# The third group's depthwise convolution moved from GpSimd to TensorE, in three parts, and the first context moved behind the second keys' transposes

## The reference

```python
q = einsum('oc,bchw->bohw', wq, fmap)                        # 64 -> 128 channels
kdw = conv_general_dilated(fmap, wdw, 3x3, pad 1, groups=C)  # depthwise, 9 taps
kv = einsum('oc,bchw->bohw', wpw, kdw)
k, v = split(kv, 2, axis=1)
q = softmax(q, over the 16 channels of a head) * 16 ** -0.5
k = softmax(k, over the 256 pixels)
context = einsum('bnd,bne->bde', k, v)
out = gelu(einsum('bnd,bde->bne', q, context))
return einsum('oc,bchw->bohw', wout, out) + bout[None, :, None, None]
```

## Time and profile before

| | |
|---|---|
| median of three runs | 659.12 us |
| profiled execution | 653.08 us, span 651.3 us |
| TensorE busy | 582.6 us, 89% of the span |
| VectorE busy | 402.6 us, 62% |
| ScalarE busy | 313.8 us, 48% |
| GpSimd busy | 292.3 us, 45% |
| mean granted TensorE clock | 0.937 |

### The profile page before, as it was taken

One profiled execution on the slowest core, in us unless ns is written; L12 is line 12 of the kernel. 1 busy time (PEld: TensorE's weight loads), 2 busy tenths in 40 slices (PEclk: granted clock), 3 DMA queues, 4 the chain that ended last, 5 costly groups with the idle time before them and its releaser, 6 DMA issues.

```text
span 651.3 us, 10438 instructions
## 1 busy us (share of the span) xinstructions
PE 582.6 (89%) x3574; PEld 303.7 (47%) x3574; DVE 402.6 (62%) x1162; ACT 313.8 (48%) x549; POOL 292.3 (45%) x371
## 2 busy tenths in 40 slices
PE   7888794898799999999998787998999999997883
PEld 6675433793232333332334557982333333467652
DVE  6655597666687766866867826744953333445567
ACT  3334675184333343344345635465555555335384
POOL 6601705150253455697697940540425243435263
PEclk9999887588999999999999978999999999997696
DMA  4720000020554424324321000024322232000001
GB/s 118 140 39 2 2 0 2 9 57 5 133 130 103 99 65 111 84 67 117 78 64 34 0 2 1 11 53 124 79 65 65 66 86 44 1 2 2 2 1 66
DMA packets 33045, 34.62 MB, mean 53 GB/s; under 512 B 11304, under 2 KB 20544, under 8 KB 32928
## 3 DMA queue, kind: packets, MB, share of 16 engines
q1 hardware_dynamic: 32992, 33.95, 22.6%
HBM read 32.50 MB, written 1.44 MB: 52 GB/s over the span
## 4 chain that ended last, share of the span: by engine, by line
PE 74%; DVE 13%; POOL 5%; issue 3%; ACT 3%; DMA 1%; SPq 0%; DVEq 0%; ACTq 0%; POOLq 0%
PE ps L1812 10%; PE ps L1849 9%; PE ps L2473 9%; PE ps L2463 8%; PE ps L1804 8%; PE ps L421 4%; PE ps L2573 2%; DVE ST L487 2%; POOL dw_out L1562 2%; PE ps L763 1%; PE ps L2882 1%; PE ps L1202 1%; POOL tap_prod L1572 1%; PE ps L2185 1%; PE ps L1362 1%
## 5 line engine op out<-in xcount | busy, mean ns | idle before, releaser
L1465 POOL TENSOR_TENSOR out_acc<-out_acc,tok_tmp 128x512 f32<-128x512 f32 x88 | 113.7, 1292 | 180.9 <-DVE tok_tmp L1677 90.5
L1744 ACT ACTIVATE act_pair<-ps 128x1024 f32<-128x1024 f32 x64 | 65.5, 1024 | 112.6 <-PE ps L1804 112.6
L1812 PE MATMUL ps<-tokP,w_raw 64*128 64x512 f32 x256 | 73.1, 648 | 1.0 <-DVE tok_split L1671 0.5
L1804 PE MATMUL ps<-tokP,w_raw 64*128 64x512 f32 x256 | 67.4, 603 | 2.4 <-ACT act_pair L1744 2.4
L2463 PE MATMUL ps<-tokP,w 64*128 64x512 f32 x256 | 63.8, 616 | 0.0
L1677 DVE TENSOR_TENSOR tok_tmp<-ps,disp_all 128x512 f32<-128x512 f32 x60 | 41.2, 690 | 25.5 <-PE ps L1849 20.0
L532 ACT ACTIVATE U<-X,nmr,rstd 128x64 f32<-128x64 f32 x120 | 41.8, 429 | 21.1 <-POOL nmr L510 16.6
L2366 DVE SCALAR_TENSOR_TENSOR tok_tmp<-ps,b,disp_all 128x512 f32<-128x512 f32 x28 | 21.0, 750 | 48.4 <-PE ps L2473 39.7
L1671 DVE TENSOR_TENSOR tok_split<-act_pair,ps 128x1024 f32<-128x1024 f32 x32 | 39.1, 1221 | 14.7 <-PE ps L1812 14.4
L2418 ACT ACTIVATE hid_four<-ps,b 128x1024 f32<-128x1024 f32 x32 | 33.9, 1110 | 29.5 <-PE ps L2463 29.5
L1671 DVE TENSOR_TENSOR hid_four<-act_pair,ps 128x1024 f32<-128x1024 f32 x32 | 39.1, 1222 | 13.9 <-PE ps L1812 12.4
(11 more groups left out here) (474 smaller groups left out, 1045.1 us busy)
## 6 DMA issues: line engine op xcount, KB each, us to landing
disp_all<-disp_dram SPq DMA_DIRECT2D x44, 512.0 KB, 6.5
w_raw<-in_L_ffn_w SPq DMA_DIRECT2D x4, 512.0 KB, 9.6
disp_all<-disp_dram SPq DMA_DIRECT2D x4, 384.0 KB, 4.9
XIN<-in_x SPq DMA_DIRECT2D x4, 256.0 KB, 3.3
w_raw<-in_L_ffn_W SPq DMA_DIRECT2D x2, 512.0 KB, 6.1
out<-XIN SPq DMA_DIRECT2D x4, 256.0 KB, 2.2
fc_raw<-in_L_conv_upfc_w SPq DMA_DIRECT2D x1, 512.0 KB, 4.6
w<-in_L_ffn_w SPq DMA_DIRECT2D x1, 512.0 KB, 10.3
```

The source lines that it names most:

```text
L1465: pool.tensor_tensor(out_acc[i % 2][:, :], out_acc[i % 2][:, :], weighed[p % 2], ALU.add).then_inc(mm["acc"].sem, 1)
L1744: act.activation(act_pair[n % 2][:, :], ps[:, 0:2, :].rearrange("p r s -> p (r s)"), ACT.Silu).then_inc(mm["act"].sem, 1)
L1804: last = pe.matmul(ps[:, r, :], w12_raw[half(r), 0, e, :], tokP[half(r), i * CHUNK:(i + 1) * CHUNK], start=True, stop=True)
L1812: last = pe.matmul(ps[:, 2 + r, :], w12_raw[half(r), 1, e, :], tokP[half(r), i * CHUNK:(i + 1) * CHUNK], start=True, stop=True)
```

## The change

Group 2's convolution leaves GpSimd: the 17 steps of `dw_pool(pool, G - 2, n)` go, and `chunk_rstd` follows the experts' last addition directly. TensorE does group 2's nine taps in three parts of 3, 2 and 4 taps, into bank 6. ScalarE moves the sum between the last two `chunk_norm` (`conv_move(G - 2)`), and `keys(2)` waits for that move. Since bank 6 also takes the context, `context(0)` now waits for the move, and stands behind `k_tr(1)`. Group 3's nine taps stand in one piece behind `q_tr(0, 1)`, after `keys(2)` and `values(2)`. The eight matmuls of `keep_clock` go.

```diff
             add_weighed(pool, e1, E1, between, count=G)
-            for n in range(5):
-                dw_pool(pool, G - 2, n)
             for i in (NCHUNK - 2, NCHUNK - 1):
                 chunk_rstd(pool, i, eps_c, m["d_var"], m["d_rstd"])
-            for n in range(5, DW_STEPS):
-                dw_pool(pool, G - 2, n)
...
-                       (G, "d_o_ps d_g d_y_ps d_xo x5"), (3, "d_hm"), (G - 1, "d_kd"), (1, "d_cw d_cv_ps d_kl"), (2 * G, "d_qt_ps d_qt"),
+                       (G, "d_o_ps d_g d_y_ps d_xo x5"), (3, "d_hm"), (G - 2, "d_kd"), (1, "d_cw"), (2, "d_cv_ps d_kl"), (2 * G, "d_qt_ps d_qt"),
...
+            def conv_move(g):
+
+                act.wait_ge(*m["d_cv_ps"](g - 1))
+                act.activation(dw_out[:, g, :], ps[:, 6, :], ACT.Copy).then_inc(m["d_kl"].sem, 1)
+
...
-            for i in (NCHUNK - 2, NCHUNK - 1):
-                chunk_norm(act, i, m["d_rstd"], m["d_u"])
+            chunk_norm(act, NCHUNK - 2, m["d_rstd"], m["d_u"])
+            conv_move(G - 2)
+            chunk_norm(act, NCHUNK - 1, m["d_rstd"], m["d_u"])
...
-            act.wait_ge(*m["d_cv_ps"](1))
-            act.activation(dw_out[:, G - 1, :], ps[:, 6, :], ACT.Copy).then_inc(m["d_kl"].sem, 1)
+            conv_move(G - 1)
...
-                pe.wait_ge(*(m["d_kd"](g + 1) if g < G - 1 else m["d_kl"](1)))
+                pe.wait_ge(*(m["d_kd"](g + 1) if g < G - 2 else m["d_kl"](g - 1)))
...
                 if g == 0:
-                    pe.wait_ge(*m["d_xp"](G - 1))
+                    pe.wait_ge(*m["d_kl"](1))
                 elif g == 1:
-                    pe.wait_ge(*m["d_kl"](1))
+                    pe.wait_ge(*m["d_kl"](2))
...
             values(0)
+            dw_tensor(G - 2, 0, 3)
             experts_back(pe, e1, E1, G - 1)
             k_tr(0)
             q_logits(1)
+            dw_tensor(G - 2, 3, 5)
             keys(1)
             values(1)
-            context(0)
+            dw_tensor(G - 2, 5, 9)
             q_tr(0, 0)
             k_tr(1)
+            context(0)
             pe.wait_ge(*e1["ta"](G + 1))
             pe.wait_ge(*m["d_qt"](1))
             d_tr(pe, G - 1)
             q_logits(2)
-            pe.wait_ge(*m["d_c"](1))
-            keep_clock(pe, 6, 8)
-            q_tr(0, 1)
-            dw_tensor(G - 1, 0, 4)
             keys(2)
             values(2)
-            dw_tensor(G - 1, 4, 9)
+            q_tr(0, 1)
+            pe.wait_ge(*m["d_c"](1))
+            dw_tensor(G - 1, 0, 9)
             context(1)
```

## The result

The changed kernel takes 651.85 us (median of 22 runs, 647.82 to 655.61). The kernel before took 654.13 us (22 runs on the same chip, 651.18 to 660.80); the median of 659.12 that the forecast started from was that of three runs and lay 5.0 us above this one. The ratio is 0.9948, 95% interval 0.9923 to 0.9974: a gain of 3.4 us, between 1.7 and 5.0, where 5.8 was forecast. The difference of the two medians is 2.3 us, that of the two means 3.7 (655.67 and 651.93). The profiled execution took 650.62 us, at a mean granted clock of 0.935 (before: 653.08 at 0.937).

A forecast was written before the change was run, and what follows sets the result against it. GpSimd's convolution of group 2 was taken to bound the stretch before `keys(2)`. 2.7 us from the clock plus 3.1 from GpSimd's wait, less what was added, gave 5.8: 659.12 - 5.8 = 653.3 us, range 651.0 to 656.3.

The forecast's parts named there:

- The stage: From `values(0)` to `context(1)`, rebuilt at full clock: `keys(2)` at 369.3, `context(1)` at 380.3 instead of 386.19, 5.8 us sooner.
- 2.7 come from the clock: From 376.31 to 385.45 TensorE took 9.14 us for work that is 6.41 at full clock.
- From there on the two programs are alike: Behind the start of `context(1)`: nothing differs, so the 5.8 us gained there reach the end.
- the dense order: TensorE's work up to `context(1)`: the forecast's other term, GpSimd's wait less what was added, 3.1 us.
- The argument on the border: Idle 2.10 us ahead of 362.86 brought no clock fall, so the 3.37 us ahead of `k_tr(3)` is near the border.
- The second fall: Rival: the clock fall behind the idle stretch ahead of `k_tr(3)` stays away, 1.7 us more gained, 651.6 us; 15%.
- The waits: Rival: delays on ScalarE's list up to `keys(2)` and in TensorE's list leave 3 to 4 us, about 656 us; 17%.
- the dense stretch: Slower rival: TensorE at 1.2 GHz from `keys(2)` on, 10.1 us more, `context(1)` at 390.4, 663.4 us; 3%.
- The gain reached the end: Rival denied this: something other than this chain gates the next stage, time stays at 659.1 us; 3%.
- GpSimd beside VectorE: Bias additions now beside `q_norm(0)` and `q_center(1)`: a neighbour may cost 0.60 us or nothing; taken as nothing.
- in direction, not in size: L1938's one 1.84 us against its median 1.24, compared with the exclusion rule's possible wait of 1.24 us.
- ScalarE free: After `v_move(2)` and `k_exp(2)`, ahead of group 3's move: free at 378.5, 1.1 us ahead of the taps' end.

The follow-up runs named there:

- before_full: Kernel before with fillers ahead of `k_tr(3)`, behind `context(0)` and behind group 3's first four taps, six routing fillers moved behind the bias products: 649.50 us, ratio 0.9906.
- after_hold: Changed kernel with 13 filler matmuls in the idle 3.38 us between `q_tr(2, 0)` and `k_tr(3)`: 647.72 us, ratio 0.9933 to the kernel before.
- after_both: Changed kernel with 13 filler matmuls ahead of `k_tr(3)` and six routing fillers moved behind the second run of bias products: 647.95 us, ratio 0.9874 to the kernel before.
- after_pool_busy: Changed kernel in which GpSimd still runs the 17 convolution steps, into a spare tile nothing reads: 651.24 us, ratio 0.9956 to the kernel before.
- after_gate: Changed kernel with only six routing fillers moved behind the second run of bias products: 646.96 us, ratio 0.9906 to the kernel before.
- before_filled: Kernel before with 15 filler matmuls behind group 3's first four taps, in the idle 3.75 us ahead of `keys(2)`: 654.85 us, ratio 1.0019.
- before_again: Kernel before run and traced once more, with no edit: ratio 1.0005 to the kernel before.
- before_gate: Kernel before with only six routing fillers moved behind the second run of bias products: 652.99 us, ratio 0.9974.

## Why the prediction was off

**The stage: right.** Forecast and measured starts: `v_move(1)` 360.9 and 361.08; `keys(2)` 369.3 and 369.53; `context(1)` 380.3 and 380.65; `k_tr(3)` 392.9 and 393.15. The clock was full from 350 to 386 us, nothing was idle above 0.78 us, and nine taps took 7.90 us, as priced from the earlier trace rows.

**The step that failed: "2.7 come from the clock", together with "From there on the two programs are alike".** The programs are alike, their clocks are not. I read the first fall of the earlier trace rows as a price that the kernel before pays and the new one does not, and took the clock behind `context(1)` for the same in both. Each of the seven traces of the two unedited kernels has two falls or more (the rows with none are before_full, and after_hold, after_both and after_pool_busy):

| | falls, start in us | sum |
|---|---|---|
| before, four traces | 374.9, 398.8; 375.0, 398.9, 426.2; 365.0, 378.7, 399.1; 363.6, 377.3, 397.8 | 85.7; 90.7; 84.8; 84.7 |
| before, none | none | 81.6 |
| after, three traces | 394.4, 421.7; 394.0, 421.3; 392.2, 419.5 | 82.0; 82.0; 82.1 |
| after, none | none | 78.7 to 78.9 |

Falls cost the kernel before 3.1 to 4.1 us in this part, 9.1 once, and the changed kernel 3.2 to 3.3, three times alike. The changed kernel's are the old fall behind the idle stretch ahead of `k_tr(3)` (1.6: after_gate has it alone, 80.4 against 78.8) and one in the routing that the first trace of before doesn't have (1.6 again: 82.0 against 80.4). So the term put at 2.7 us measured 0 to 1 us against three of the four traces of before, and 5.9 against the fourth. With the 2.8 of the dense order the three make 3 to 4, and the ratio says 3.4 (1.7 to 5.0). The two agree, but one doesn't prove the other. before_filled is the same statement from the other side.

**Where the runs of the whole program differ.** Nine of the 22 runs of before lie above 657 us (mean 659.4) and the other 13 between 651.2 and 655.6 (mean 653.1); of the 22 of after none is above 655.61 (mean 651.9). So 2.6 of the 3.7 us between the means are these nine runs, and against the other 13 the gain is 1.1 us. The one traced execution of before above 657 (before_again, 659.30) is the one with the third fall, which cost 4.9 us (19.6 against 14.7). Whether that fall makes all nine isn't shown; nor what the slower runs of after meet, since none of its three traced executions was above its median.

**The argument on the border** ("the idle 2.10 us ahead of 362.86 brought no such fall") was drawn from one trace. The third and fourth of the kernel before have a fall there, and so have before_filled and before_gate.

**The baseline.** That the forecast of 653.3 us is near 651.85 is luck: 659.12 was 5.0 us too high for 22 runs (its three runs are among the nine above 657 us), and the gain taken from it was too large. The profiled execution, 653.08, had been the better guide; from 654.13 the same 5.8 us would have given 648.3.

**The rivals.** The second fall did not stay away: it came in all three traces of after. The waits did not eat half: `keys(2)` was 0.2 us late. The clock did not fall in the dense stretch. The gain reached the end, in part. The rival with the right size of gain, "about 656 us" for half the gain, had the wrong mechanism.

**GpSimd beside VectorE.** I took nothing for it, and nothing it was. After, the bias additions moved into VectorE's work and paid themselves:

```profile
363.17 1.23 DVE L1934 TENSOR_TENSOR q_buf<-q_buf,qr 128x1024 f32<-128x1024 f32 x1
```

```profile
L2298 POOL TENSOR_TENSOR X<-X,b_o x4: 1267/1280/2321, 360.7 to 367.1; 128x512 f32<-128x512 f32 x4
```

One of the four, which lay beside this product, took 2.32 us; the others took about 1.27, and the four of before 1.24 on the average. VectorE's product kept its 1.23. By the Trainium skill's rule (SBUF — State Buffer, "Who interferes with whom") the two exclude each other for the whole instruction. In this run the waiting was on GpSimd's side; with more of GpSimd's work beside it, in after_pool_busy, it was on VectorE's too (1.88, and 1.25 for four columns). Both agree with the rule, and neither was on the path. In after_pool_busy the four-column product ran from 356.90 to 358.15, and the GpSimd addition beside it from 356.86 to 358.12. The 1.84 us of before, for which the prediction found agreement "in direction, not in size", fit in size too: a GpSimd addition had begun 0.5 us earlier (367.67, for 1.28 us) and had 0.76 us to go.

**Left open.** What makes an execution meet a fall at one place and not another isn't shown: after_pool_busy, and after_hold in the routing, met none where after met them three times. Nor is it shown why the clock in the stage from L2849 to L2885 was higher in after_gate than in the others.

**Two small slips in the working.** ScalarE free is 375.6 + 0.91 + 1.81 = 378.3, not 378.5, and the slower rival's 390.4 is 4.2 us behind 386.19, which gives 663.3. Neither bears on the forecast.

## What to carry to other kernels

A slow stretch that comes from TensorE's clock is not a cost of the edit's place alone. Read it in several executions, and compare the two orders with every idle or thin stretch filled; what is left there is what the change itself is worth. When work is pulled forward, look at every idle or thin stretch behind it, untouched code included. Filling the idle 3.38 us ahead of `k_tr(3)` took a fall away in all three kernels that did it and made nothing later; moving six fillers to where the products are thin cost nothing, and what it gains needs more traces.

## What was not expected of the hardware

The clock fell where TensorE had no idle time: in 413 to 429 us the profile has it busy for 16.00 of 16.00 us at a clock of 0.89, and the fall began at 421.7, behind sixteen records of one column and eight of 16 columns. With twelve filler records between the two, none of four traces has a fall there; without them six of twelve have one. Twelve records of 128 columns took 2.77 us in it, 1.50 outside.

In the 22 runs of the changed kernel the time followed the mean granted clock, from 647.8 us at 0.946 to 655.6 at 0.932 (a line through all of them gives 6.8 us for that difference, about 0.5 for each thousandth, and accounts for two thirds of the variance). So most of the spread of this kernel's time goes with the clock. Between the two kernels the mean clock is no such guide: the profiled executions had 0.937 and 0.935, and the one with the lower clock was faster by 2.5 us.
